# State space scan: half of each state's product with C moved from VectorE to TensorE and ScalarE

## What is computed

```python
x = jnp.einsum('ed,bld->bel', in_proj_w, hidden_states)
u = jax.nn.silu(conv(x) + conv_b)
x_dbl = jnp.einsum('ke,bel->bkl', x_proj_w, u)
dt_lo, Bm, Cm = x_dbl[:, :DR], x_dbl[:, DR:DR + DS], x_dbl[:, DR + DS:]
delta = jax.nn.softplus(jnp.einsum('er,brl->bel', dt_proj_w, dt_lo) + dt_proj_b)
def step(state, xs):
    d_t, B_t, C_t, u_t = xs
    dA = jnp.exp(d_t[..., None] * A)
    state = state * dA + (d_t * u_t)[..., None] * B_t[:, None, :]
    y_t = jnp.einsum('ben,bn->be', state, C_t)
    return (state, y_t)
y = (ys + D[None, :, None] * u) * jax.nn.silu(z)
```

## Time and profile before

| | |
|---|---|
| median of the runs shown | 4288.86 us |
| profiled execution, its time | 4301.73 us |
| profiled execution, its span | 4299.9 us |
| this stage | from 2805 to 3560 us of the span |
| VectorE busy, whole span | 72% |
| TensorE busy, whole span | 93% |
| ScalarE busy, whole span | 53% |

### The profile page before, as it was taken

How to read it: one execution, slowest core, us unless ns; L and a number is a source line. 1 busy time by engine, 2 the same in 40 slices (tenths; PEclk the granted TensorE clock), 3 DMA queues, 4 the chain that set the end, 5 groups by cost and what they waited for, 6 DMA issues and landing times. The chain is left out here.

```text
span 4299.9 us, 179869 instructions
## 1 busy us (share of the span) xinstructions
PE 4000.7 (93%) x76866; PEld 2486.6 (58%) x76866; DVE 3105.3 (72%) x5135; ACT 2296.8 (53%) x6321; POOL 933.6 (22%) x1927
## 2 busy tenths in 40 slices
PE   7999999999999999999999999757879789999998
PEld 4667767767676676767667676522333334444443
DVE  4788888888888888888888887478999991212221
ACT  4577776676676667676676766444344331111110
POOL 1333333333333333333233333100000000000000
PEclk8999999999999999999999999778989899999999
DMA  2222222222221212212122221142323332000000
GB/s 76 65 60 71 65 69 68 58 76 66 63 68 59 77 52 75 70 56 78 57 70 70 63 71 49 41 148 72 94 83 96 92 121 89 29 1 30 0 20 10
DMA packets 133721, 277.31 MB, mean 64 GB/s; under 512 B 21004, under 2 KB 62496, under 8 KB 129472
## 3 DMA queue, kind: packets, MB, share of 16 engines
q1 hardware_dynamic: 132784, 265.60, 20.2%
q10 hardware_dynamic: 144, 0.20, 0.0%
HBM read 235.07 MB, written 30.67 MB: 62 GB/s over the span
## 5 line engine op out<-in xcount | busy, mean ns | idle before, releaser
L420 PE MATMUL a_pb<-a_x_t,a_w_qkv 128*128 128x512 f32 x1536 | 844.0, 641 | 15.5 <-DMA a_x_t<-in_x_t 8.2
L1318 DVE TENSOR_TENSOR a_nq<-a_nq,a_tot 128x1024 f32<-128x1024 f32 x320 | 392.8, 1227 | 133.9 <-PE a_pb L451 85.2
L1281 DVE SCALAR_TENSOR_TENSOR a_acc<-a_pb,a_taps,a_acc 128x511 f32<-128x511 f32 (+2 forms) x576 | 425.5, 739 | 31.1 <-ACT a_acc L866 17.4
L2119 PE MATMUL m_p_y<-m_h,k_ident_sb 128*128 128x512 f32 x512 | 285.4, 710 | 130.7 <-DVE m_h L2356 130.7
L2830 DVE TENSOR_TENSOR a_x_t<-f_gate,f_pb 128x512 f32<-128x512 f32 x128 | 88.0, 687 | 383.1 <-ACT f_gate L2754 383.1
L2754 ACT ACTIVATE f_gate<-f_pb 128x512 f32<-128x512 f32 x132 | 78.8, 597 | 411.7 <-PE f_pb L2695 275.4
L420 PEld LDWEIGHTS a_pb<-a_x_t,a_w_qkv 128*128 128x128 f32 x1536 | 241.1, 192 | 99.0 <-issue 67.4
L451 PEld LDWEIGHTS a_pb<-a_nq,a_ks 128*32 128x32 f32 x20480 | 214.3, 111 | 143.3 <-issue 112.8
L2350 DVE TENSOR_TENSOR_SCAN m_h<-m_da,m_h 128x2048 f32<-128x2048 f32 x64 | 283.1, 4424 | 17.7 <-ACT m_da L2262 12.4
L1718 POOL COPY a_apt<-a_apt_fine 32x256 f32<-32x256 f32 x256 | 100.5, 393 | 882.4 <-DVE a_apt_fine L1336 857.8
L2119 PEld LDWEIGHTS m_p_y<-m_h,k_ident_sb 128*128 128x128 f32 x512 | 112.7, 228 | 295.1 <-DVE m_h L2356 161.9
(11 more groups left out here) (332 smaller groups left out, 8841.6 us busy)
## 6 DMA issues: line engine op xcount, KB each, us to landing
a_rows<-rows SPq DMA_DIRECT2D x192, 512.0 KB, 3.9
a_amp_sums<-amp_sums SPq DMA_DIRECT2D x64, 508.0 KB, 3.7
attn_o<-a_o_out SPq DMA_DIRECT2D x64, 256.0 KB, 2.7
m_b_rows<-ssm_bc SPq DMA_DIRECT2D x64, 256.0 KB, 3.7
m_c_rows<-ssm_bc SPq DMA_DIRECT2D x64, 256.0 KB, 4.5
k_big<-attn_o SPq DMA_DIRECT2D x16, 1024.0 KB, 8.3
a_w_qkv<-in_w_qkv SPq DMA_DIRECT2D x48, 256.0 KB, 3.2
k_big<-in_w_gu SPq DMA_DIRECT2D x3, 1536.0 KB, 13.3
```

The lines of the kernel that those rows point to most:

```text
L420: mm = nc.tensor.matmul(pb[:, V_BANK if i == P_V else KQ_BANK], w_qkv[:, i, k], x_t[:, k, b * T:(b + 1) * T], start=(k == 0), stop=(k == D ...
L1281: last = nc.vector.scalar_tensor_tensor(acc[:, i, d:T], src[:, 0:T - d], taps[:, i, 3 - d:4 - d], acc[:, i, d:T], ALU.mult, ALU.add)
L1318: last = nc.vector.tensor_tensor(part, part, spread(blocks, list(part.shape)), ALU.mult)
L2119: nc.tensor.matmul(p_y[:, et], ident[:], h[:, (b * DS + n) % 3, et], start=(n == 0), stop=(n == DS - 1), skip_group_check=True).then_inc(s ...
```

## The change

Tiles 0 and 1 (`SIDE` = 2) are multiplied with C on VectorE as before. Tiles 2 and 3 (`TURNED` = 2) take another way. TensorE transposes the scanned tile into a new PSUM bank `p_h` (`turn_h`, four transposes), so that tokens lie on the partitions; ScalarE scales each block of 128 tokens by C, which is now one number for a partition (`scale_h`, four instructions, into `h_turned_c`); TensorE adds the result to `p_y` with the identity (`sum_turned`). After the 16 rows ScalarE copies the two sums out (`keep_y`), TensorE turns them back (`turn_y`), and `finish` waits for that. C with tokens on the partitions, `c_token`, is made once for a batch element by `turn_c` and `keep_c`. `p_x` has one PSUM bank instead of two, and `ROWS` goes from 3 to 2; the B load now waits for `times_b` (`dbu_ready`) instead of `times_c`. The four `DT` matmuls are spread over steps 36 to 42. ScalarE issues a row's decays in pairs, at the first two steps of a row, each pair ahead of a `scale_h`.

```diff
-        ROWS, LEAD = 3, 4
+        ROWS, LEAD = 2, 4
+        SIDE = 2
+        TURNED = ET - SIDE
...
-        p_x = ps("p_x", (P, 2, T))
+        p_x = ps("p_x", (P, T))
+        p_h = ps("p_h", (P, T))
...
+                sp.dma_start(x_dbl[DR + DS:], io["ssm_bc"][0, DS:]).then_inc(c_rows_in, 16)
...
                         if k >= ROWS:
+                            sp.wait_ge(dbu_ready, k - ROWS + 1)
+                        sp.dma_start(b_rows[:, k % ROWS], spread(io["ssm_bc"][b, n:n + 1], [P, T])).then_inc(b_in[k % ROWS], 16)
+                        if k >= ROWS:
                             sp.wait_ge(cs_ready, k - ROWS + 1)
-                        sp.dma_start(b_rows[:, k % ROWS], spread(io["ssm_bc"][b, n:n + 1], [P, T])).then_inc(b_in[k % ROWS], 16)
...
+                def turn_h(row, et):
+
+                    q = row * TURNED + et - SIDE
+                    pe.wait_ge(scanned, row + 1)
+                    if q:
+                        pe.wait_ge(h_scaled, q)
+                    pe.wait_ge(c_token_ready, tokens_before(row))
+                    for tt in range(TT):
+                        mm = nc.tensor.transpose(p_h[:, tt * P:(tt + 1) * P], h[:, row % 3, et, tt * P:(tt + 1) * P], ident[:])
+                    mm.then_inc(h_turned, 1)
+
+                def sum_turned(row, et):
+
+                    b, n = divmod(row, DS)
+                    if n == 0 and b:
+                        pe.wait_ge(y_ready, (b - 1) * ET + et + 1)
+                    pe.wait_ge(h_scaled, row * TURNED + et - SIDE + 1)
+                    nc.tensor.matmul(p_y[:, et], ident[:], h_turned_c[:, et - SIDE],
+                                     start=(n == 0), stop=(n == DS - 1), skip_group_check=True).then_inc(summed, 1)
...
-                        if i % ET == 1 and b * N + i > ET:
-                            for et in range(ET):
-                                sum_state(b * N + i - 1 - ET + et)
+                        before_row = b * DS + i // ET - 1
+                        if before_row >= 0 and i % ET == 0:
+                            turn_h(before_row, SIDE)
...
+                        if before_row >= 0:
+                            if i % ET == 1:
+                                turn_h(before_row, SIDE + 1)
+                            if i % ET == 2:
+                                for et in range(SIDE):
+                                    sum_state(before_row * ET + et)
+                            if i % ET >= ET - TURNED:
+                                sum_turned(before_row, i % ET)
...
+                def scale_h(row, et):
+
+                    b, n = divmod(row, DS)
+                    act.wait_ge(h_turned, row * TURNED + et - SIDE + 1)
+                    act.wait_ge(c_token_ready, b + 1)
+                    if n == 0 and b:
+                        act.wait_ge(y_turned, (b - 1) * TURNED + et - SIDE + 1)
+                    elif row:
+                        act.wait_ge(summed, (row - 1) * ET + et + 1)
+                    for tt in range(TT):
+                        last = nc.scalar.activation(h_turned_c[:, et - SIDE, tt * P:(tt + 1) * P], p_h[:, tt * P:(tt + 1) * P],
+                                                    ACT.Copy, scale=c_token[:, b % 2, tt, n:n + 1])
+                    last.then_inc(h_scaled, 1)
...
-                        if b * N + i + LEAD < B * N:
-                            decay(b * N + i + LEAD)
+                        if b * N + i + LEAD < B * N and i % ET < 2:
+                            for et in range(2):
+                                decay(b * N + i + LEAD + i % ET + et)
+                        before_row = b * DS + i // ET - 1
+                        if before_row >= 0 and i % ET < TURNED:
+                            scale_h(before_row, SIDE + i % ET)
...
-                    nc.vector.tensor_tensor(h[:, row % 3], h[:, row % 3], spread(c_rows[:, row % ROWS:row % ROWS + 1], [P, ET, T]),
+                    nc.vector.tensor_tensor(h[:, row % 3, 0:SIDE], h[:, row % 3, 0:SIDE],
+                                            spread(c_rows[:, row % ROWS:row % ROWS + 1], [P, SIDE, T]),
                                             ALU.mult).then_inc(cs_ready, 1)
```

More of the change, by code:

```diff
@@ L1937, in o_step, with flips_before_c, tokens_before @@
             return divmod(i - O_START, O_SHORT) if b == 0 else divmod(i, O_SPAN)
+        def flips_before_c(b):
+            at = [i for i, step in PE_STEPS.items() if step == C_TOKEN][0]
+            rows = (b - 1) * DS + at // ET - 1
+            return rows * TURNED + min(at % ET, TURNED)
+        def tokens_before(row):
+            at = [i for i, step in PE_STEPS.items() if step == C_TOKEN][0]
+            return min(1 + (row + 1) // DS + (1 if (row + 1) % DS > at // ET else 0), B)
         def ahead(b, i, steps):
@@ L2048, in project, with turn_y @@
+                def turn_y(b, et):
+                    pe.wait_ge(y_kept, b * TURNED + et - SIDE + 1)
+                    for tt in range(TT):
+                        mm = nc.tensor.transpose(p_y[:, et, tt * P:(tt + 1) * P], h_turned_c[:, et - SIDE, tt * P:(tt + 1) * P],
+                                                 ident[:])
+                    mm.then_inc(y_turned, 1)
                 def project(b, tt, head):
@@ L2143, in _ @@
                             rank(0)
-                for j in range(B * N - ET, B * N):
-                    sum_state(j)
+                for et in range(SIDE):
+                    sum_state(B * N - ET + et)
+                for et in range(SIDE, ET):
+                    turn_h(B * DS - 1, et)
+                for et in range(SIDE, ET):
+                    sum_turned(B * DS - 1, et)
+                for et in range(SIDE, ET):
+                    turn_y(B - 1, et)
                 for lt in range(TT):
@@ L2276, in _ @@
                     decay(j)
+                keep_c(0)
                 for b in range(B):
                     for i in range(N):
[L2279 to L2280 removed]
+                        if b * N + i + LEAD < B * N and i % ET < 2:
[4 more added lines that the diff above has]
+                            scale_h(before_row, SIDE + i % ET)
+                        if b and i == ET - 1:
+                            for et in range(SIDE, ET):
+                                keep_y(b - 1, et)
                         if b == 0 and 4 <= i < 12 and i % 2 == 0:
@@ L2297, in _ @@
                             keep_x2_t(b - 1, (i - TURN_X - 3) // 3)
+                for et in range(SIDE, ET):
+                    scale_h(B * DS - 1, et)
+                for et in range(SIDE, ET):
+                    keep_y(B - 1, et)
                 keep_rank(1)
```

99 lines of the change are left out of this document (69 added, 30 removed).

## The result

| | before | changed |
|---|---|---|
| median, 5 runs each | 4288.86 us (4282.43 to 4297.2) | 4321.92 us (4311.68 to 4327.38) |
| ratio, 95% interval | | 1.007 [1.0046, 1.0093] |
| profiled execution, span | 4299.9 us | 4310.7 us |
| this stage in it | 755.4 us | 778.2 us |
| batch elements 0, 1, 2 (scan to scan) | 190.8, 179.9, 181.6 us | 191.4, 186.0, 188.2 us |

By the medians the change makes the kernel 33 us slower; I had forecast 34 us faster. The stage's length is taken from VectorE's first instruction in it to its first in the next stage, in the one profiled execution of each kernel.

The account below looks back on a forecast made before the run. VectorE was taken to set the pace, TensorE a close second. Terms of -10, -14.3, -14.3, -14 and +1.4 gave -51 us, less 17 for half clock -34: 4254.5 us against the median 4288.86, range 4228 to 4300.

Parts of the forecast that it names:

- The saving: VectorE's times_c at half size: 1.07 us less for each of 64 rows, 68.5 us, bounds 67 and 73.
- In rows 0 to 6 and 12 to 15 the same count gives none.: Middle batch elements: step-by-step count finds no stall in these rows; TensorE's longest rows stand beside other VectorE work.
- has room: ScalarE: a row takes about 5.2 us against VectorE's new pitch of 7.84; busy about 100 to 120 us an element.
- The count of rows 7 to 11: Middle batch elements, TensorE counted step by step: stall 9.0 us in place of 6.2, each element saving 14.3 us.
- P(n) + 3.4: Earliest start of scan(n+1), P(n) being TensorE's start of row n; decays stand behind scale_h and turn_h.
- The start: Batch element 0: with ROWS = 2 scan(2) waits for a late B load, 7.4 us later.
- the 13.3 us less for rows 3 to 12: Batch element 0: scan(13) 109.2 us after scan(3), against 122.50 us before.
- The end: After the last scan: times_c 2.3 us less, then turns, scalings, sums, keep_y, turn_y before finish; net +1.4 us.
- Element 3: Last batch element, without DBL and DT: stall 4.5 us at rows 12 and 13, saving 14 us.
- The half-clock allowance: TensorE stretches at half clock, 3.4 us each: one in each of elements 1 to 3, two in element 0; 17 us.
- The second rival: TensorE's clock falls and it becomes the bound: at 0.76, about 4315 us, slower; chance 0.12.
- The third rival: Coupling costs twice the count, through ScalarE's long pieces and late B rows: 4287 us, no change; chance 0.20.

Follow-up runs that it names:

- the repairs: Changed kernel with taps at a row's first step, sums one step earlier and B of row 2 loaded early: 4271.6 us, ratio 0.9977.
- g_start: Changed kernel with taps at a row's first step, sums one step earlier, B of row 2 loaded ahead of x_rows: 4271.6 us, ratio 0.9977, stage 745.2 us.
- f_both: Changed kernel with taps at a row's first step, ahead of decays and scale_h, and sums one step earlier: 4283.5 us, ratio 0.9994, stage 753.5 us.
- e_side4: Changed kernel with SIDE = 4, no tile turned, every other edit kept: 4273.9 us, ratio 0.9965, stage 742.4 us.
- e_quarter: Changed kernel with only one of a turned tile's four blocks transposed, a pricing run: 4294.7 us, ratio 1.002, stage 763.7 us.
- i_one: g_start with scale_h as one 128x512 activation instead of four scalings, a pricing run: 4268.6 us, ratio 0.9972, stage 744.1 us.

## Why the prediction was wrong

- **The saving, right.** 68.5 forecast, 68.3 measured on VectorE. By the stage the forecast was 34 us less and 22.8 more came out, 57 us over it.
- **The step that failed**: "In rows 0 to 6 and 12 to 15 the same count gives none." The count followed the decays behind `scale_h` and left out what else stands in ScalarE's order there: the taps. Their waits of 39.6 us lie in rows 2 to 6 of elements 0 to 2, three in each. Rows 16 to 22 took 83.5 us before, 88.6 in the changed kernel and 80.0 with the repairs. I had written that ScalarE "has room". It had, by busy time; room doesn't help an instruction that stands behind one that waits for another engine. Moving the taps took 19.5 us off the stage, taps and sums together 24.7, and this is shown. Of the 57 us that leaves 32 for the points below.
- **The count of rows 7 to 11, right in mechanism, short in size.** I said scan(n+1) starts no earlier than P(n) + 3.4. In g_start `turn_h` starts at 3063.33 and the scan at 3066.41, and at 3084.70 and 3087.73: 3.1 and 3.0 us. But the waits for decays and sums of rows 7 to 11 in element 1, to the scan of row 12, came to 17.6 us in the changed kernel and 16.9 in f_both, where I had 9.0. The largest is at row 12's scan, 5.5 us in f_both. Most of it is not from `scale_h`: in e_side4 4.4 us stand there too. Two of its decays stand behind the softplus step (a 128x2048 activation of 1.91 us), and that behind the last of the spread `DT`. In my count the `DT` pair cost TensorE about 1 us and the scan nothing.
- **The gain that I didn't see.** The sums behind the heads, 13 us, is in the order that I had printed. It partly hid the loss: against the same kernel with nothing turned, the turned tiles cost 36 us.
- **The start, right.** scan(2) 7.0 us later (41.0 after the stage's start against 34.0), forecast 7.4, behind a B row as said. But the 13.3 us less for rows 3 to 12 failed: from scan(3) to scan(13) it was 122.5 before and 121.0 after, with tap waits of up to 9.2 us, where I had 109.2. From the stage's start to scan(16) element 0 should have saved 10 in all; it lost 1.3.
- **The end**: +4.5 us, forecast +1.4. `finish` waits 4.9 us for the sums and 4.4 for `turn_y`.
- **Element 3**: forecast 14 less, measured 4.3 more for rows 48 to 63. It has no taps. Its waits are sums, decays, and 6.7 us for the norm's deviation, a ScalarE instruction behind `scale_h` like the tap. None of the repairs moved it. In g_start:

```profile
3383.15 1.14 ACT L2307 ACTIVATE m_h_turned_c<-m_p_h,m_c_token 128x128 f32<-128x128 f32 x4 [1.51 <-PE m_p_h L2098]
3384.31 1.28 ACT L2319 ACT_TABLE_LOAD   x1
...
3385.94 0.18 DVE L2522 RECIPROCAL m_stats<-m_stats 128x4 f32<-128x4 f32 x1 [6.11 <-ACT m_stats L2319]
```

With nothing turned VectorE does not wait there. The count left it out for the same reason as the taps.

- **The half-clock allowance** of 17 us wasn't needed (and it was too large: 8 sum records in 6.08 us instead of 3.70 are 2.4 us lost, not 3.4). The second rival (clock 0.76, 4315 us) had the right side, and a time near the measured one, for a wrong reason: PEclk is 0.94 to 0.96. In the runs here, transposes mixed among matmuls cost the clock nothing: 1.00 in the stretch of g_start above, with 164 PE records, many of them transposes. With three quarters of them left out it is lower: 0.90 in element 1 of e_quarter, 0.94 in the changed kernel. The rule that transposes don't count as activity (the Trainium skill, "TensorE: Matmul & The Clock Gate", PE-mode transpose), by which the prediction worked out that rival's time, is not borne out by this mix; here the measurement decides.
- **The third rival** was nearest in mechanism (ScalarE's and TensorE's orders coupled) but I priced it at twice my own count, 32 us. It came to 67 over my forecast by the median and 57 by the stage, and its B rows were not late: after the start no B row is waited for by more than 1 us in the changed kernel.

Left open: the scan's waits for decays, 41.9 us in g_start, which no edit removed without a loss elsewhere; what it would give to move the norm's deviation ahead of `scale_h`; and why the changed kernel's median has 10 us outside the stage. A form that turns tiles only in rows where TensorE has room was not tried, since a tile's sums in `p_y` must all have the same layout.

## What to carry to other kernels

An instruction that waits for another engine makes everything behind it wait too, however idle its engine is. So when a change puts a cross-engine wait into an in-order queue, go through every step number of that engine, ask who consumes what stands behind the wait and how much lead there is; the busy share says nothing about it. Count a gain on the bounding engine only for the stretches where it is the bound: here TensorE is full in rows 7 to 11 with the sums reordered and without a single transpose. And take a change apart into its edits even when it is a loss: its reordering of the sums and an early B load, without its main idea, make the fastest complete kernel here, 4261.4 us, ratio 0.9946 [0.9926, 0.9966].

## What the runs showed of the hardware

- A `turn_h` of four float32 128x128 transposes takes TensorE 0.43 us from its start to the next matmul's (3020.30 to 3020.73), and ScalarE starts on it 0.63 us after its first. The scaling of four 128x128 blocks is 1.14 us; one 128x512 instruction in its place takes 0.68 us (684 ns in i_one), and made no difference once the queue was right.
- The granted clock rose with more transposes, 0.92 to 0.94 in element 1, while TensorE's waits for `times_c` fell from 130.7 to 41.8 us in the stage. With three quarters of the transposes left out again (e_quarter) it was 0.90, with 58.1 us of these waits.
